# Causal mask of an attention: added by VectorE while it finds the row maxima, in place of mask matmuls on TensorE

## The chip, the core and the metric

The kernel runs on one core of one Trainium2 chip. The metric is the device time of one execution in microseconds (us). The core has four computing engines that each work through their own list of instructions in order, and wait for one another by semaphores: TensorE (PE in the profile: matmuls, and its weight loads as PEld), VectorE (DVE), ScalarE (ACT), GpSimd (POOL). DMA queues are fed by SyncE (SP) and by GpSimd. TensorE writes only to PSUM; the other data lie in SBUF.

## The reference, cut to what matters

One decoder layer on x (8 batches x 512 rows x 256 columns): a first attention without softmax, then a causal attention with 16 heads of 64, then 16 experts with 4 chosen per row. The change is in the second:

```python
qh = (q @ Wq.T + bq)...; kh = (k @ Wk.T + bk)...; vh = (v @ Wv.T + bv)...   # b, 16 heads, 512, 64
scores = einsum('bhqd,bhkd->bhqk', qh, kh) / sqrt(64)
causal = tril(ones((512, 512), bool))
scores = where(causal, scores, -inf)
attn   = softmax(scores, axis=-1)
out    = einsum('bhqk,bhkd->bhqd', attn, vh) ...  @ Wo.T + bo
```

## The kernel before

The whole layer is one program. It has three stages: the first attention (to about 209 us of the span), the causal attention (to about 1131 us), and the experts (to the end). The change is in the causal attention.

**Pairs.** The causal attention goes over 64 pairs of heads (8 batches, 8 pairs each; n counts the pairs). The two heads of a pair are called even and odd. The 512 rows of a head are four tiles of 128 rows; row tile i needs only the first (i+1)*128 columns of scores. The tiles are taken in blocks, `BLOCKS = (3, 2, 1)`: block 3 is row tile 3 (512 columns), block 2 is row tile 2 (384), block 1 is row tiles 1 and 0 (256 and 128).

**Order.** `attention_plan` writes out one list of steps, and every engine goes through that list and takes its own part of each step. For a pair n the list is, in short: scores of blocks 3 and 2; the transposes ("turn", five groups of four, L1286) of the probabilities of pair n-1, with "soften" of blocks 3 and 2 between them; "even" of blocks 3 and 2; the projections of k, v and q for pair n+1; scores and soften of block 1; steps of the routing or of the next batch ("middle"); "even" of block 1; further steps ("second"); "weigh" (probabilities times v, L1298) and "keep" of pair n-1. Then the scores of pair n+1 follow.

**One block on the engines.** "scores" (TensorE, L1269): six matmuls per row tile, since each product is made of three terms with high and low parts, for two heads; then four mask matmuls (L1274), in which an identity and a mask (zero on and below the diagonal, -1e30 above it, both bf16, held twice for the two halves of the array) add the mask to the last 128 columns in PSUM. "soften": VectorE finds the negated row maxima of both heads in one `tensor_reduce` per row tile (L1526), straight from PSUM; ScalarE takes the exponentials from PSUM with that bias, writes them to `prob` in SBUF and collects the row sums (L1400, one per head and row tile, each with an instruction that reads the accumulator). "even": VectorE inverts the sums (L1533) and scales `prob` in place (L1538). The transposes of pair n wait for "even" of block 1 of pair n (signal `s_norm`).

**Banks.** Scores use two PSUM slots `SB` of two banks, in turn: block after block. Before the change the scores of a block wait until the exponentials of the block two before have been read out (`s_exp`). All other products share four `work` banks, each free again when VectorE or ScalarE has emptied it.

**Around it.** k and q of a pair are split in a high part (ScalarE, L1383 and L1385) and a low part (VectorE, L1515 and L1519) before their scores. In some pairs VectorE has more between soften and even of block 1: `norm3` (L1485) in pair 2 of a batch, `place` (L1642 to L1657) and `lower_x` (L1508) in pair 6. In the first attention VectorE copies identity and mask into their two halves (`repeat_halves`, L748 and L749).

## Time and profile before

| | |
|---|---|
| time, median of 3 runs | 1635.06 us (1634.19 to 1638.66) |
| span of the profiled execution | 1636.8 us |
| PE busy | 1574.4 us (96%) |
| PE weight loads busy | 1329.4 us (81%) |
| DVE busy | 1164.3 us (71%) |
| ACT busy | 1077.0 us (66%) |
| POOL busy | 524.1 us (32%) |
| mask matmuls, L1274 | 1024 |
| row maxima, L1526 | 256, 198.1 us busy |
| exponentials, L1400 | 512, 265.9 us busy, and 512 accumulator reads, 108.8 us |

The profile gives no other time for the profiled execution than its span; it lies between the lowest and the highest of the three runs, 1.7 us over their median. "Busy" adds up the durations of instructions; on TensorE neighbouring matmuls overlap, so what one of them costs is read from start to start and not from its own duration.

### The profile page before, as it was taken

To read this page: it belongs to the slowest core of one execution; us is meant where nothing else is said; L and a number is where in the kernel's file an instruction comes from. 1 tells how busy PE (TensorE), PEld (TensorE's weight loads), DVE (VectorE), ACT (ScalarE), POOL (GpSimd) and SP (SyncE) were. 2 spreads that over 40 slices of the span, in tenths; PEclk is the share of its full clock that TensorE was granted. 3 is DMA by queue.
4 is the path that set the end of the run, shared out by engine and by line. 5 is a ranking of instruction groups with operands and counts; after the bars stand their busy time and mean duration, and the time that the engine had idled before them with its cause. 6 is when DMAs were issued, how large, how long until landed. Compare 5 with 4: busy or idle time off the path is not lost.

```text
span 1636.8 us, 35892 instructions
## 1 busy us (share of the span) xinstructions
PE 1574.4 (96%) x12438; PEld 1329.4 (81%) x12438; DVE 1164.3 (71%) x2745; ACT 1077.0 (66%) x2702; POOL 524.1 (32%) x440
## 2 busy tenths in 40 slices
PE   5999989999999999999999999997999999999997
PEld 4888867777777777777777777776999999999997
DVE  6877767676767677677677777777886666666663
ACT  3555557666766676676676667666776677677675
POOL 3444400000310300301202102104567745655655
PEclk9999999999999999999999999999999999999999
DMA  3122194044292490580730302046778887777874
GB/s 102 39 90 78 40 267 127 1 130 144 72 286 67 143 272 11 174 250 18 227 111 36 101 1 80 15 136 205 162 182 206 200 200 173 175 181 171 176 180 49
DMA packets 164610, 216.14 MB, mean 132 GB/s; under 512 B 16672, under 2 KB 124752, under 8 KB 164432
## 3 DMA queue, kind: packets, MB, share of 16 engines
q1 hardware_dynamic: 134080, 173.77, 35.2%
q0 software_dynamic: 28896, 38.62, 12.7%
q8 instruction: 103, 1.69, 0.4%
q10 hardware_dynamic: 1456, 1.44, 0.3%
q14 instruction: 75, 0.61, 0.1%
HBM read 90.76 MB, written 123.03 MB: 131 GB/s over the span
## 4 chain that ended last, share of the span: by engine, by line
PE 69%; ACT 14%; DVE 11%; issue 4%; DMA 1%; POOL 0%; SPq 0%; DVEq 0%; ACTq 0%
PE ex_H L1836 14%; PE ex_Y L1850 13%; ACT xa_prob L1400 7%; PE xa_work L1315 6%; PE xa_work L1240 5%; PE xa_work L1298 5%; PE xa_S L1269 5%; PE xa_work L1286 5%; PE xa_work L1251 4%; ACT xa_probT L1414 4%; PE a_work L458 4%; PE ex_X L1818 2%; DVE xa_nmax L1526 2%; DVE xa_prob L1538 2%; ACT xa_probT L1411 1%
## 5 line engine op out<-in xcount | busy, mean ns | idle before, releaser
L1400 ACT ACTIVATE xa_prob<-xa_S,xa_nmax 128x512 f32<-128x512 f32 (+3 forms) x512 | 265.9, 534 | 115.2 <-DVE xa_nmax L1526 97.6
L1943 POOL DMA_INDIRECT out<-ex_y,ahead_bits x158 | 272.8, 1727 | 200.7 <-POOLq L1939 73.6
L1836 PE MATMUL ex_H<-ex_xT,ex_w 128*128 128x256 f32 x1896 | 245.8, 286 | 5.9 <-issue 3.2
L1836 PEld LDWEIGHTS ex_H<-ex_xT,ex_w 128*128 128x128 f32 x1896 | 231.5, 191 | 6.8 <-issue 6.7
L1850 PE MATMUL ex_Y<-experts_w_hi,ex_hT 128*128 x1264 | 236.6, 280 | 0.2 <-issue 0.2
L1526 DVE TENSOR_REDUCE xa_nmax<-xa_S 128x2 f32<-128x1024 f32 (+3 forms) x256 | 198.1, 816 | 4.7 <-PE xa_S L1274 4.7
L1850 PEld LDWEIGHTS ex_Y<-experts_w_hi,ex_hT 128*128 128x128 f32 x1264 | 198.7, 188 | 0.5 <-issue 0.5
L1711 POOL DMA_INDIRECT expert_rows<-kept_xn,kept_rows x112 | 111.1, 992 | 266.6 <-DVE xa_prob L1538 224.2
L1921 DVE TENSOR_TENSOR ex_hT<-ex_h,ex_hT 128x512 fp32r<-128x512 f32 x158 | 108.2, 692 | 120.4 <-ACT ex_hT L1875 116.6
L1414 ACT ACTIVATE xa_probT<-xa_work 128x512 f32<-128x512 f32 x256 | 139.6, 603 | 81.9 <-PE xa_work L1286 73.4
L1850 PE MATMUL ex_Y<-experts_w_lo,ex_hT 128*128 x632 | 176.3, 279 | 0.0
L1538 DVE TENSOR_SCALAR xa_prob<-xa_prob,xa_sums 128x512 f32<-128x512 f32 (+3 forms) x512 | 169.3, 384 | 6.8
L1870 ACT ACTIVATE ex_h<-ex_H,kept_b 128x256 f32<-128x256 f32 x316 | 131.2, 466 | 63.6 <-DVE kept_b L1909 47.8
L1286 PE MATMUL xa_work<-ahead_ident,xa_prob 128*128 128x128 f32 x1280 | 155.4, 277 | 8.5 <-DVE xa_prob L1538 7.1
L1298 PE MATMUL xa_work<-xa_probT,xa_v 128*64 128x512 f32 (+3 forms) x1024 | 153.5, 442 | 2.2 <-ACT xa_probT L1411 2.2
L1286 PEld LDWEIGHTS xa_work<-ahead_ident,xa_prob 128*128 128x128 f32 x1280 | 139.4, 142 | 15.8 <-DVE xa_prob L1538 10.2
L1298 PEld LDWEIGHTS xa_work<-xa_probT,xa_v 128*64 128x64 f32 x1024 | 68.2, 137 | 82.9 <-issue 67.0
L1883 ACT ACTIVATE ex_y<-ex_Y,ahead_bits 128x256 f32<-128x256 f32 x158 | 73.9, 473 | 77.4 <-PE ex_Y L1850 57.0
L1533 DVE RECIPROCAL xa_sums<-xa_sums 128x2 f32<-128x2 f32 (+1 forms) x192 | 32.1, 167 | 128.4 <-ACT xa_prob L1400 128.3
L1850 PEld LDWEIGHTS ex_Y<-experts_w_lo,ex_hT 128*128 128x128 f32 x632 | 118.6, 188 | 0.0
L1400 ACT ACTIVATION_READ_ACCUMULATOR xa_prob<-xa_S,xa_nmax 128x1 f32 x512 | 108.8, 213 | 0.0
L1875 ACT ACTIVATE ex_hT<-ex_h 128x512 fp32r<-128x512 f32 x158 | 99.9, 632 | 5.0
(384 smaller groups left out, 3587.6 us busy)
## 6 DMA issues: line engine op xcount, KB each, us to landing
expert_rows<-xa_room_of_w_hi_and SPq DMA_DIRECT2D x256, 273.0 KB
kept_x<-expert_rows SPq DMA_DIRECT2D x52, 273.0 KB
ex_w_raw<-in_w SPq DMA_DIRECT2D x27, 512.0 KB
ahead_ctx<-in_w SPq DMA_DIRECT2D x26, 512.0 KB
ahead_x<-in_w SPq DMA_DIRECT2D x26, 512.0 KB
kept_xn<-expert_rows SPq DMA_DIRECT2D x27, 273.0 KB
experts_w_lo<-in_w SPq DMA_DIRECT2D x6, 1024.0 KB, 5.5
expert_rows<-xa_room_of_w_hi_and SPq DMA_DIRECT2D x32, 136.5 KB
```

The costliest lines, as they stand in the source:

```text
L1286: m = pe.transpose(PJ[:, col:col + P], prob[n % 2][:, odd, PROB_AT[i] + j * P:PROB_AT[i] + (j + 1) * P], ident[:])
L1298: m = pe.matmul(OB[HD * odd:HD * odd + HD, j * P:512], v[n % 2][:, j, first_col + HD * odd:first_col + HD * odd + HD], probT[:, odd, PROB_ ...
L1400: m = act.activation(prob[n % 2][:, odd, PROB_AT[i]:PROB_AT[i] + width], SB[slot[at]][:, odd, col:col + width], ACT.Exp, bias=nmax[n % 2][ ...
L1414: act.activation(probT[:, odd, first_col:first_col + 512], bank(step, at)[:], ACT.Copy).then_inc(t_ev.of(at), 1)
L1526: m = dve.tensor_reduce(nmax[n % 2][:, i, :], SB[slot[at]][:, :, SCORE_COL[i]:SCORE_COL[i] + (i + 1) * P], AX.X, ALU.max, negate=True)
L1538: m = dve.tensor_scalar(part, part, sums[n % 2][:, i, odd:odd + 1], None, ALU.mult)
L1711: pool.indirect_dma_start(rows_dram, bass.IndirectOffsetOnAxis(rows_i[b % 2][:, t, k:k + 1], 0), xn3[:, t, :], None).then_inc(scattered[of ...
L1836: m = pe.matmul(bank[:, (f % 2) * ROWS:(f % 2 + 1) * ROWS], ww[:, c, f * P:(f + 1) * P], xx[:, c, :], start=(i == 0), stop=(i == len(terms ...
L1850: m = pe.matmul(YB[a][:, 0:D], hh[:, f, a * P:(a + 1) * P], W2[:, bass.ds(own * WE + f * D, D)], start=(i == 0), stop=(i == len(terms) - 1))
L1870: i = act.activation(h32[:, f, :], HB[2 * (j % 2) + u][:, (f % 2) * ROWS:(f % 2 + 1) * ROWS], ACT.Gelu, bias=b1[j % 2][:, f:f + 1])
L1921: dve.tensor_tensor(hT[j % 2][1][:, fs, :], h32[:, fs, :], f32(hT[j % 2][0][:, fs, :]), op=ALU.subtract).then_inc(h_lo.of((j, u)), 1)
L1943: pool.indirect_dma_start(out, bass.IndirectOffsetOnAxis(tail[j % NT][:, a, 0:1].bitcast(I32), 0), y[j % NY][:, a, :], None, compute_op=AL ...
```

## The change

TensorE no longer adds the mask: the four mask matmuls of each row tile go, and the third term's matmul ends the group. The mask is now one bf16 tile of 128 x 512 that is zero but for its last 128 columns; a row tile of some width takes the last `width` columns of it. "soften" on VectorE becomes one `tensor_tensor_reduce` per head and row tile (8 per pair, in place of 4 reductions): it reads the scores from PSUM and the mask from SBUF, writes -(score + mask) to `prob`, and gives the minimum over the row, which is the negated maximum. ScalarE then takes the exponentials in place in `prob`, in SBUF, with scale -1. The PSUM slot is free when VectorE is through (`s_max`), not when ScalarE is. `s_pe` and `s_max` are waited for head by head. The identity and mask copies of the first attention go; GpSimd fills one mask.

```diff
-        self.ident_of, self.mask_of, self.tri, self.onesb = (self.bits[:, at, :] for at in (slice(0, 2), slice(2, 4), 4, 5))
+        self.mask, self.tri, self.onesb = self.bits[:, 0:N_TILES, :].rearrange("p t n -> p (t n)"), self.bits[:, 4, :], self.bits[:, 5, :]
...
-            def repeat_halves():
-                w.wait_ge(mask_set, "maskb")
-                for odd in range(2):
-                    for half_ in range(2):
-                        mine, theirs = slice(HD * odd, HD * odd + HD), slice(HD * half_, HD * half_ + HD)
-                        dve.tensor_copy(ahead.ident_of[mine, half_, :], identb[theirs])
-                        i = dve.tensor_copy(ahead.mask_of[mine, half_, :], maskb[theirs])
-                i.then_inc(halves_set.of(0), 1)
+            def scale_bq():
                 w.wait_ge(small_in, "rb")
...
+            pool.affine_select(out=ahead.mask[:, S - P:S], in_=ahead.mask[:, S - P:S], compare_op=ALU.is_ge, fill=NEG, base=0,
+                               pattern=[[-1, P]], channel_multiplier=1).then_inc(mask_set.of("mask"), 1)
...
+        mask_of, tri, onesb = lambda width: ahead.mask[:, S - width:S], ahead.tri, ahead.onesb
...
                 if at in before_in_slot:
-                    w.wait_ge(s_exp, (*before_in_slot[at], 1))
+                    w.wait_ge(s_max, (*before_in_slot[at], 1))
...
-                            pe.matmul(bank_pair[:, odd, col:col + n_cols], qq[mine, i * P:(i + 1) * P], kk[mine, 0:n_cols],
-                                      start=(term == 0), stop=False)
-                    for half in range(2):
-                        for odd in range(2):
-                            mine, skipped = slice(HD * odd, HD * odd + HD), HD * half
-                            m = pe.matmul(bank_pair[:, odd, col + width - P + skipped:col + width], ident_of[mine, half, :],
-                                          mask_of[mine, half, skipped:P], start=False, stop=(half == 1))
-                            if half == 1 and i == ROWS_OF[blk][-1]:
+                            m = pe.matmul(bank_pair[:, odd, col:col + n_cols], qq[mine, i * P:(i + 1) * P], kk[mine, 0:n_cols],
+                                          start=(term == 0), stop=(term == 2))
+                            if term == 2 and i == ROWS_OF[blk][-1]:
                                 m.then_inc(s_pe.of((n, blk, odd)), 1)
...
             elif step == "soften":                      # ScalarE
                 n, blk = at
-                w.wait_ge(t_pe, (n - 2, len(TURNS) - 1), n >= 2)
-                w.wait_ge(s_norm, (n - 2, 1), n >= 2)
-                w.wait_ge(Wo_lo, 0, n == 1)
-                w.wait_ge(s_max, at)
+                w.wait_ge(s_inv, (n - 2, 1), n >= 2)
                 for odd in range(2):
+                    w.wait_ge(s_max, (n, blk, odd))
                     for i in ROWS_OF[blk]:
-                        col, width = SCORE_COL[i], (i + 1) * P
-                        m = act.activation(prob[n % 2][:, odd, PROB_AT[i]:PROB_AT[i] + width],
-                                           SB[slot[at]][:, odd, col:col + width], ACT.Exp,
-                                           bias=nmax[n % 2][:, i, odd:odd + 1], accum_out=sums[n % 2][:, i, odd:odd + 1])
+                        part = prob[n % 2][:, odd, PROB_AT[i]:PROB_AT[i] + (i + 1) * P]
+                        m = act.activation(part, part, ACT.Exp, scale=-1.0, bias=nmax[n % 2][:, i, odd:odd + 1],
+                                           accum_out=sums[n % 2][:, i, odd:odd + 1])
...
             elif step == "soften":                      # VectorE
                 n, blk = at
                 w.wait_ge(s_exp, (n - 2, 1, 1), n >= 2)
-                w.wait_ge(s_pe, (n, blk, 1))
-                for i in ROWS_OF[blk]:
-                    m = dve.tensor_reduce(nmax[n % 2][:, i, :], SB[slot[at]][:, :, SCORE_COL[i]:SCORE_COL[i] + (i + 1) * P],
-                                          AX.X, ALU.max, negate=True)
-                m.then_inc(s_max.of(at), 1)
+                w.wait_ge(t_pe, (n - 2, len(TURNS) - 1), n >= 2)
+                w.wait_ge(Wo_lo, 0, n == 1)
+                for odd in range(2):
+                    w.wait_ge(s_pe, (n, blk, odd))
+                    for i in ROWS_OF[blk]:
+                        col, width = SCORE_COL[i], (i + 1) * P
+                        m = dve.tensor_tensor_reduce(prob[n % 2][:, odd, PROB_AT[i]:PROB_AT[i] + width],
+                                                     SB[slot[at]][:, odd, col:col + width], mask_of(width), scale=-1.0, scalar=-NEG,
+                                                     op0=ALU.add, op1=ALU.min, accum_out=nmax[n % 2][:, i, odd:odd + 1])
+                    m.then_inc(s_max.of((n, blk, odd)), 1)
```

Line numbers of the kernel after are lower by 8 to 17 in the causal attention. On TensorE, block 1 of one pair stands so before (`xa_S` are the scores in PSUM, `ahead_bits` holds identity and mask):

```order
L1269 MATMUL xa_S<-xa_k0hi,xa_q0lo 128x256 x2
L1269 MATMUL xa_S<-xa_k0lo,xa_q0hi 128x256 x2
L1269 MATMUL xa_S<-xa_k0hi,xa_q0hi 128x256 x2
L1274 MATMUL xa_S<-ahead_bits 128x128 x2
L1274 MATMUL xa_S<-ahead_bits 128x64 x2
L1269 MATMUL xa_S<-xa_k0hi,xa_q0lo 128x256 x2
L1269 MATMUL xa_S<-xa_k0lo,xa_q0hi 128x256 x2
L1269 MATMUL xa_S<-xa_k0hi,xa_q0hi 128x256 x2
L1274 MATMUL xa_S<-ahead_bits 128x128 x2
L1274 MATMUL xa_S<-ahead_bits 128x64 x2
```

and so after:

```order
L1260 MATMUL xa_S<-xa_k0hi,xa_q0lo 128x256 x2
L1260 MATMUL xa_S<-xa_k0lo,xa_q0hi 128x256 x2
L1260 MATMUL xa_S<-xa_k0hi,xa_q0hi 128x256 x2
L1260 MATMUL xa_S<-xa_k0hi,xa_q0lo 128x256 x2
L1260 MATMUL xa_S<-xa_k0lo,xa_q0hi 128x256 x2
L1260 MATMUL xa_S<-xa_k0hi,xa_q0hi 128x256 x2
```

Only the mask matmuls are gone; the rest keeps its order. On VectorE, in pair 6 of a batch, the stretch from the low part of q to the inverse sums of block 1 stands so before (`xa_nmax` are the negated maxima, `xa_pos` to `kept_rows` is the step `place`):

```order
L1519 SCALAR_TENSOR_TENSOR xa_q1lo<-xa_work,ahead_bqT,xa_q1hi 128x512
L1526 TENSOR_REDUCE xa_nmax<-xa_S 128x2 x2
L1642 TENSOR_TENSOR xa_pos<-xa_work,routing_count 128x64
L1645 TENSOR_TENSOR routing_count<-xa_work,routing_count 128x16
L1647 TENSOR_TENSOR xa_key<-xa_pos,ahead_ebase 128x64
L1650 TENSOR_TENSOR xa_key<-xa_key,xa_mask 128x64
L1653 MAX xa_key<-xa_key 128x8 x4
L1657 TENSOR_SCALAR kept_rows<-xa_key 128x16
L1508 TENSOR_TENSOR ahead_xT_lo<-xa_work,ahead_xT_hi 128x512
L1533 RECIPROCAL xa_sums<-xa_sums 128x4
```

and its beginning after:

```order
L1502 SCALAR_TENSOR_TENSOR xa_q1lo<-xa_work,ahead_bqT,xa_q1hi 128x512
L1513 ISA xa_prob,xa_nmax<-xa_S,ahead_bits 128x256
L1513 ISA xa_nmax 128x1
L1513 ISA xa_prob,xa_nmax<-xa_S,ahead_bits 128x128
L1513 ISA xa_nmax 128x1
L1513 ISA xa_prob,xa_nmax<-xa_S,ahead_bits 128x256
L1513 ISA xa_nmax 128x1
L1513 ISA xa_prob,xa_nmax<-xa_S,ahead_bits 128x128
L1513 ISA xa_nmax 128x1
L1630 TENSOR_TENSOR xa_pos<-xa_work,routing_count 128x64
```

Two reductions have become four `tensor_tensor_reduce`, and each of these is followed by an instruction of its own that writes only the 128x1 result. So soften of a pair has 16 instructions on VectorE where it had 4. ScalarE and GpSimd have the same order as before in this stage.

## Rows read from the trace of the kernel before

**Rows 1.** Stretch: length; busy PE, PEld, DVE, ACT, POOL; clock; DMA share; GB/s.
```profile
440.00:610.00 170.00, 168.35 (x1339) 126.92 (x1338) 123.80 (x313) 114.75 (x311) 30.76 (x31) 1.00 0.64 190
```

**Rows 2.** Waits of TensorE, whole span: us in total, times, longest us.
```profile
PE xa_work L1286 <- DVE xa_prob L1538: 7.1, 20, 1.0
```

**Rows 3.** Chain that ended last, from 712 us: start us, us, what.
```profile
718.33 0.10 PE xa_S L1274 x4
718.43 1.60 PE xa_work L1286 x13
```

**Rows 4.** The same chain, one pair from 240 us.
```profile
241.95 1.09 ACT xa_probT L1414 x2
...
248.85 0.75 DVE xa_q1lo L1519
249.60 0.94 DVE xa_nmax L1526 x2
...
250.56 1.73 ACT xa_prob L1400 x8
...
252.53 1.02 DVE xa_prob L1538 x4
...
253.59 0.67 PE xa_work L1286 x4
```

**Rows 5.** The same chain in pair 6 of a batch.
```profile
644.97 0.93 DVE xa_nmax L1526 x2
...
647.28 0.59 DVE ahead_xT_lo L1508
...
647.99 1.01 DVE xa_prob L1538 x4
```

**Rows 6.** Timeline of VectorE: start us, us, instructions, [idle before <- releaser].
```profile
646.66 0.41 DVE L1653 MAX8 xa_key<-xa_key 128x8 f32<-128x16 f32 x4
647.10 0.18 DVE L1657 TENSOR_SCALAR kept_rows<-xa_key 128x16 int32<-128x16 f32 x1
647.19 0.68 DVE L1508 TENSOR_TENSOR ahead_xT_lo<-xa_work,ahead_xT_hi 128x512 fp32r<-128x512 f32 x1
647.79 0.17 DVE L1533 RECIPROCAL xa_sums<-xa_sums 128x4 f32<-128x4 f32 x1
```

**Rows 7.** VectorE's groups by form: count, busy us, mean ns of one.
```profile
L1526 DVE TENSOR_REDUCE xa_nmax<-xa_S 128x2 f32<-128x1024 f32 x64 | 77.8, 1216 | 1.2 <-PE xa_S L1274 1.2
L1526 DVE TENSOR_REDUCE xa_nmax<-xa_S 128x2 f32<-128x256 f32 x64 | 26.6, 416 | 0.0
L1593 DVE MATCH_VALUE_LOAD xa_repl<-xa_top,ahead_probs 128x8 f32 x32 | 2.7, 85 | 0.3
```

**Rows 8.** ScalarE's groups by form.
```profile
L1400 ACT ACTIVATION_READ_ACCUMULATOR xa_prob<-xa_S,xa_nmax 128x1 f32 x512 | 108.8, 213 | 0.0
L563 ACT ACTIVATE a_sq<-a_sq_q 128x256 f32<-128x256 f32 x32 | 13.4, 418 | 1.0
L560 ACT ACTIVATE a_sq_q<-a_work 128x256 f32<-128x256 f32 x32 | 11.9, 372 | 0.0
```

**Rows 9.** Timeline of VectorE and TensorE at the turn of pairs.
```profile
717.10 1.01 DVE L1538 TENSOR_SCALAR xa_prob<-xa_prob,xa_sums 128x256 f32<-128x256 f32 x4
...
660.38 1.01 DVE L1538 TENSOR_SCALAR xa_prob<-xa_prob,xa_sums 128x256 f32<-128x256 f32 x4
...
662.13 2.08 PE L1286 MATMUL xa_work<-ahead_ident,xa_prob 128*128 128x128 f32 x17
```

**Rows 10.** Timeline of VectorE in pair 2 of a batch.
```profile
701.92 1.38 DVE L1485 TENSOR_SCALAR kept_xn<-xa_x,xa_ln_mv,xa_ln_rstd 128x256 f32<-128x256 f32 x4
703.79 0.18 DVE L1533 RECIPROCAL xa_sums<-xa_sums 128x4 f32<-128x4 f32 x1 [0.49 <-ACT xa_prob L1400]
```

**Rows 11.** Chain in the first attention: the first and last copy of the two halves.
```profile
70.27 0.09 DVE ahead_bits L748
...
71.28 0.10 DVE ahead_bits L749
```

More of the change, by code:

```diff
@@ L132, in __init__ @@
         self.b1 = [sb(f"b1_{i}", [P, FC]) for i in range(2)]
-        bits, wide = ahead.bits[:].rearrange("p a b -> p (a b)").bitcast(F32), RT * (PAY - D)
-        self.b1T, self.scr = bits[:, 0:E * FC], bits[:, 2 * P:2 * P + 6 * E].rearrange("p (i e) -> p i e", e=E)
-        self.tail = [bits[:, E * FC + i * wide:E * FC + (i + 1) * wide].rearrange("p (a c) -> p a c", a=RT) for i in range(NT)]
+        room, wide = ahead.bits[:].rearrange("p a b -> p (a b)").bitcast(F32), RT * (PAY - D)
+        self.b1T, self.scr = room[:, 0:E * FC], room[:, 2 * P:2 * P + 6 * E].rearrange("p (i e) -> p i e", e=E)
+        self.tail = [room[:, E * FC + i * wide:E * FC + (i + 1) * wide].rearrange("p (a c) -> p a c", a=RT) for i in range(NT)]
 class Tables:
@@ L305, in first_attention @@
         ones, half = sb("ones", [P, 2]), sb("half", [P, N_TILES])
-        identb, maskb = sb("identb", [P, P], BF16), sb("maskb", [P, P], BF16)
         b2, b2_hi = sb("b2", [P, D]), sb("b2_hi", [P, D], F32R)
@@ L362, in first_attention @@
         b2_zero, b2_in = signal("b2_zero", [0]), landed("b2_in", range(len(GATE_AT)))
-        b2_ready, halves_set = signal("b2_ready", ["cast", "hi", "lo"]), signal("halves_set", [0])
-        mask_set, bq_scaled, bo_added = signal("mask_set", ["fill", "identb", "maskb"]), signal("bq_scaled", [0]), signal("bo_added", [0])
+        b2_ready = signal("b2_ready", ["cast", "hi", "lo"])
+        mask_set, bq_scaled, bo_added = signal("mask_set", ["fill", "mask"]), signal("bq_scaled", [0]), signal("bo_added", [0])
         x_of = lambda b: x_in[b % 3] if b < B else ahead.x1_0
@@ L818, in vector @@
                 if b == 2:
-                    repeat_halves()
+                    scale_bq()
                 k = chunk_of(b)
@@ L892, in gpsimd @@
             pool.memset(b2[:], 0.0).then_inc(b2_zero.of(0), 1)
-            for tile, fill in ((identb, 0.0), (maskb, 0.0), (ahead.tri, 1.0), (ahead.onesb, 1.0)):
+            for tile, fill in ((ahead.mask, 0.0), (ahead.tri, 1.0), (ahead.onesb, 1.0)):
                 i = pool.memset(tile[:], fill)
@@ L943, in first_attention @@
         engines = {"tensor": tensor, "scalar": scalar, "vector": vector, "gpsimd": gpsimd, "sync": sync}
-        return engines, x1_stored, {"work_ev": work_ev, "bo_added": bo_added}
+        return engines, x1_stored, {"work_ev": work_ev, "bo_added": bo_added, "mask_set": mask_set}
 BLOCKS = (3, 2, 1)
@@ L1129, in cross_attention @@
         s_pe, s_exp = signal("s_pe", heads_of), signal("s_exp", heads_of)
-        s_max, s_inv, s_norm = (signal(n, of_scores) for n in ("s_max", "s_inv", "s_norm"))
+        s_max = signal("s_max", heads_of)
+        s_inv, s_norm = (signal(n, of_scores) for n in ("s_inv", "s_norm"))
         t_pe, t_ev = signal("t_pe", turns), signal("t_ev", turns)
```

5 lines of the change are left out of this document (removed).

## The prediction

> **What bounds the kernel now.** I read the stretches of busy time first. In the causal attention TensorE is busy 168.35 of 170 us, VectorE 123.80, ScalarE 114.75 [rows 1]. So taking work from TensorE should pay, if VectorE and ScalarE can follow. Whether they can is not in the shares, so I read TensorE's waits next: its first transpose of a pair (L1286) waited 20 times for VectorE's scaled probabilities (L1538), 7.1 us in all [rows 2]. Small, but there are only 63 such hand-overs, so at 20 of them the other two engines are already as late as TensorE. The chain of waits shows the path there: first transposes, then ScalarE from 241.95 without a pause until q is split, VectorE (low part of q at 248.85, maxima at 249.60), ScalarE (exponentials 250.56), VectorE (scaling 252.53), and the next pair's transposes at 253.59 [rows 4]. Such a pair is set by ScalarE and VectorE, not by TensorE.
>
> I sorted the 63 hand-overs by how long the probabilities had been ready when TensorE came for them; the batches repeat almost to 0.1 us. Class A, 13: TensorE waits, the chain is that of [rows 4]. Class B, 7 (pair 2 of a batch): the same, with `norm3` (L1485) on VectorE between the maxima and the inverse sums [rows 10]. Class C, 7 (pair 6, and the last pair but one): VectorE has no pause from the maxima at 644.97 through place and lower_x to the scaling at 647.99 [rows 5]. Class D, 6: ready at 717.10 + 1.01 = 718.11, wanted at 718.43 [rows 9, 3]: 0.3 us to spare. Class E, 30: at least 0.7 us to spare; the tightest is ready at 661.39 and wanted at 662.13 [rows 9].
>
> **The change part by part.**
>
> *Mask matmuls.* Four of them hold the path for 0.10 us (718.33 to 718.43) [rows 3]; their own durations overlap and say nothing. 256 row tiles make 25.6 us, 0.40 us a pair. That is all TensorE can give back. In class E all of it is gained.
>
> *Row maxima.* Two things have to be sized. A two-input instruction over 512 columns from PSUM takes 0.60 us from its start to the next start (647.19 to 647.79) [rows 6]. The slope of the present reductions is (1216 - 416) / 768 = 1.04 ns a column [rows 7]; so 0.60, 0.47, 0.33 and 0.20 us for 512, 384, 256 and 128 columns. Then the separate instruction that writes the 128x1 minimum. VectorE has no such one in this trace. The nearest are small ones: MATCH_VALUE_LOAD takes 85 ns itself [rows 7], four MAX8 take 0.44 us from start to start (646.66 to 647.10), 0.11 each [rows 6]; ScalarE's accumulator read has 213 ns [rows 8]. From below it could be hidden altogether (0), from above it is 0.21. I take 0.10, as MAX8 is an instruction of the same engine. Block 1 then needs 2 x (0.33 + 0.20) + 4 x 0.10 = 1.46 us on VectorE in place of 0.93 [rows 5]; but ScalarE may begin after one head. Before, it began 0.96 after the maxima (249.60 to 250.56) [rows 4]; now about 0.73 plus the read's tail, 0.8: 0.2 us sooner. Blocks 3 and 2 cost VectorE 2 x 1.07 + 0.4 = 2.54 us in place of 2.0; ScalarE can start block 3 some 0.07 sooner. The unknown of the sum is what one of the 8 instructions with its read costs beyond this.
>
> *Exponentials.* From SBUF in place of PSUM. A ScalarE instruction of 256 columns with an accumulator takes 418 ns from SBUF (L563) and 372 from PSUM (L560) [rows 8]: 0.045 more each, 0.18 for four. In classes A to C eight of them lie on the path of a pair, in D the last four. It could be nothing, if the difference is one of the function.
>
> *The PSUM slot* comes free after the minima and no longer after the exponentials. That helps no class by itself: in A to C the probabilities, not the slot, end the wait. The new waits of VectorE (transposes of pair n-2) and of ScalarE (inverse sums of pair n-2) are long met; behind a waiting VectorE would stand the scaling and the low parts of k and q.
>
> *The copies* in the first attention: eight, from 70.27 to 71.38 on the chain [rows 11], 1.1 us; later the chain runs into a transfer, so between 0 and 1.1; I take 0.6.
>
> Per hand-over this gives:
> - A: -0.20 (earlier start) + 0.18 + 0.18 (eight exponentials) - 0.07 = +0.09 us; 13 make 1.2 lost. TensorE's 0.40 is worth nothing here: it only waits longer.
> - B: VectorE is now late in place of ScalarE: 1.46 + 1.38 = 2.84 us from the first maximum to the inverse sums [rows 10], where ScalarE would have them after 0.8 + 1.73 + 0.18 + latency = 2.75 and before had them after 0.93 + 1.87 = 2.80 (701.92 to 703.79). +0.04 there, +0.11 in the first part of the pair: 0.15, 7 make 1.1 lost.
> - C: VectorE alone: 1.46 - 0.93 = 0.53, and 0.11 in ScalarE's part before it: 0.64, 7 make 4.5 lost.
> - D: 0.27 to spare after the latency, and 0.02 from the chain: 0.29 gained, 1.7 for 6.
> - E: 0.40, 12.0 for 30.
>
> Sum: 12.0 + 1.7 + 0.6 - 1.2 - 1.1 - 4.5 = 7.5 us gained of 25.6. The profiled execution's span of 1636.8 would become 1629.3. It stands 1.7 us over the median of the runs, so I set the gain against the median: 1635.1 - 7.5 = 1627.6 us. The experts' stage has none of these instructions and stays.
>
> The price of error is steep. For each us that an instruction with its read costs more, A and D lose 2 us a hand-over, B and C 4 (all four before the scaling): 26 + 12 + 28 + 28 = 94. So 0.08 us more each, and the gain is gone.
>
> **The rivals.**
>
> *1. Cheap minima.* The read is hidden: 0.10 less each. A gains 0.11 (1.4), B 0.14 until ScalarE is late again (1.0), C loses 0.24 (1.7), D and E 0.40 (14.4), copies 1.1: 16.2 gained, 1618.9 us. For it: ScalarE's own reads, 213 ns long, advance its chain by far less; 8 exponentials and reads take 1.73 us [rows 4]. Against: VectorE's smallest instructions all take some 0.1.
>
> *2. Everything TensorE gives back.* 63 x 0.40 + 1.1 = 26.3, 1608.8 us. It needs slack in the 20 hand-overs where TensorE waits now [rows 2]. I hardly believe it.
>
> *3. No overlap, no change.* The two instructions do not overlap as present neighbours do: 0.68 long but 0.60 to the next start [rows 6]. 0.08 each, 94 x 0.08 = 7.5 lost: 1635.1 us. The Trainium skill (VectorE: DVE Perf Modes, section The DRAIN you can't avoid) says that the next operation does not start until the pipe is empty, and advises to keep the count of operations low; by that rule alone this case would be the forecast, and it speaks against a change that makes 16 instructions of 4. The trace does not agree with it for ordinary neighbours.
>
> *4. VectorE becomes the bound.* The read costs as much as ScalarE's 0.21, and the new instruction, of a kind that the trace lacks, some 0.05 to 0.1 more than an ordinary two-input one: 0.16 to 0.21 each. 94 x 0.19 = 17.9 lost against 7.5: 1645.5 us. The place is block 1 of pairs 2 and 6 and the pairs like [rows 4]; it is slower than no change from 0.08 each, by over 0.3% from 0.13. VectorE's 16 instructions a pair stand for it; that its share would still be near 85% stands against a general jam, not against these places.
>
> *5. Half rate.* The instruction runs at two cycles a column: 1280 columns x 2 heads x 1.04 ns = 2.7 us more a pair. VectorE has 123.80 of 170 us [rows 1], 10.4 of a pair's 14.3, so it would be full, and all classes lose; roughly 30 us slower, 1665. For it nothing in the trace: its two-input instruction with one input in PSUM takes 0.60 us for 512 columns with all that is fixed in it [rows 6], which leaves no room for two cycles a column at the reductions' 1.04 ns a cycle. The Trainium skill (Vector Engine (DVE) Microarchitecture Reference, section Points that are easy to get wrong) says that a two-source instruction with an accumulator runs at half rate if both sources are non-bf16 and in SBUF; here the mask is bf16 and the scores are in PSUM, so by its own words it does not apply; no run here shows it.
>
> **How the numbers follow.** Chances: forecast 0.43, rival 1 0.17, rival 2 0.05, rival 3 0.15, rival 4 0.17, rival 5 0.03. 0.3% is 4.9 us, about what a measurement of this kernel can tell from no change. The forecast's own spread (a read of 0.06 to 0.14) is 1624 to 1631.5, so a quarter of it falls within 0.3%. Faster: 0.05 + 0.17 + 0.32 = 0.54. Same: 0.11 + 0.15 and a little of rival 4, 0.27. Slower: 0.19. The range goes from rival 1 with some of rival 2 to the middle of rival 4: 1616 to 1644.
>
> **What would show it.** Right: TensorE's waits for the scaled probabilities grow from 7.1 us to some 15 to 20, since it saves 0.4 us and gets it back in classes A to C; pairs of class E become 0.4 us shorter; the new instruction is near 0.69 and 0.29 us for 512 and 128 columns, its read near 0.15 in itself and 0.10 from start to start; exponentials 0.04 longer than before. In class C VectorE has no pause before the scaling and it comes later by 0.5 us. Wrong: first the start-to-start time of the new pair of instructions. If it is over 0.18 beyond the plain two-input one, the kernel is slower or the same. If the exponentials are not longer, A gains 0.3 a hand-over, 4 us more.

## The result and the profile after

The changed kernel takes 1611.22 us (median of 4 runs, 1608.31 to 1615.61), the kernel before in the same comparison 1635.65 us (1634.19 to 1638.66). The ratio is 0.9849, 95% interval 0.9829 to 0.9869. The forecast was 1627.6 us with a range down to 1616: the direction was right, the size was not. 24.4 us were gained where 7.5 were forecast. The profiled execution has a span of 1613.9 us against 1636.8, 22.9 us less.

The stretches of busy time after (length; busy PE, PEld, DVE, ACT, POOL; clock; DMA share; GB/s) answer to [rows 1]:

```profile
440.00:610.00 170.00, 167.44 (x1190) 127.23 (x1186) 131.14 (x472) 120.25 (x317) 28.04 (x28) 1.00 0.76 191
```

VectorE is busier (131.14 of 170 us, before 123.80), and so it is idle for less. TensorE's waits (us in total, times, longest) answer to [rows 2]:

```profile
PE xa_work L1272 <- DVE xa_prob L1526: 16.7, 28, 2.2
```

16.7 us in place of 7.1. This is inside the 15 to 20 that the forecast gave as the sign that it was right. It is no such sign: a wait grows when the awaited engines get slower, and also when TensorE gets faster by more than they do. The table of hand-overs below shows the second: where TensorE waits (A and B) the hand-overs became shorter, not longer.

VectorE's and ScalarE's new groups by form (count | busy us, mean ns of one):

```profile
L1513 DVE CUSTOM_DVE_ANT_0 xa_prob<-xa_S,ahead_bits 128x512 f32<-128x512 f32 x128 | 82.7, 683 | 1.1 <-PE xa_S L1260 1.1
L1513 DVE CUSTOM_DVE_ANT_0 xa_prob<-xa_S,ahead_bits 128x128 f32<-128x128 f32 x128 | 36.6, 286 | 0.0
L1513 DVE DVE_READ_ACCUMULATOR2_ANT xa_nmax<- 128x1 f32 x512 | 42.5, 83 | 0.0
L1384 ACT ACTIVATE xa_prob<-xa_prob,xa_nmax 128x512 f32<-128x512 f32 x128 | 91.4, 722 | 1.9 <-DVE xa_nmax L1513 1.9
L1384 ACT ACTIVATE xa_prob<-xa_prob,xa_nmax 128x128 f32<-128x128 f32 x128 | 49.6, 387 | 0.0
```

The new instruction takes 683 and 286 ns, as forecast (0.69 and 0.29). Its read takes 83 ns. What it costs the next one stands in the timeline. VectorE after, block 1 of the pair that answers to [rows 4] (start us, us, instruction):

```profile
247.60 0.75 DVE L1502 SCALAR_TENSOR_TENSOR xa_q1lo<-xa_work,ahead_bqT,xa_q1hi 128x512 fp32r<-128x512 f32 x1 [0.31 <-ACT xa_q1hi L1371]
248.27 0.41 DVE L1513 CUSTOM_DVE_ANT_0 xa_prob<-xa_S,ahead_bits 128x256 f32<-128x256 f32 x1
248.61 0.08 DVE L1513 DVE_READ_ACCUMULATOR2_ANT xa_nmax<- 128x1 f32 x1
248.61 0.28 DVE L1513 CUSTOM_DVE_ANT_0 xa_prob<-xa_S,ahead_bits 128x128 f32<-128x128 f32 x1
248.82 0.08 DVE L1513 DVE_READ_ACCUMULATOR2_ANT xa_nmax<- 128x1 f32 x1
...
249.38 0.08 DVE L1513 DVE_READ_ACCUMULATOR2_ANT xa_nmax<- 128x1 f32 x1
250.84 0.18 DVE L1521 RECIPROCAL xa_sums<-xa_sums 128x4 f32<-128x4 f32 x1 [1.37 <-ACT xa_prob L1384]
251.05 1.01 DVE L1526 TENSOR_SCALAR xa_prob<-xa_prob,xa_sums 128x256 f32<-128x256 f32 x4
```

The read starts at 248.61, and so does the next reduction. It costs no start-to-start time at all. All four take 249.38 - 248.27 = 1.11 us, where the forecast had 1.46.

ScalarE in the same block, first after and then before:

```profile
248.94 0.51 ACT L1384 ACTIVATE xa_prob<-xa_prob,xa_nmax 128x256 f32<-128x256 f32 x1 [1.37 <-DVE xa_nmax L1513]
```

```profile
250.56 0.47 ACT L1400 ACTIVATE xa_prob<-xa_S,xa_nmax 128x256 f32<-128x256 f32 x1 [1.75 <-DVE xa_nmax L1526]
```

and VectorE's maxima there before:

```profile
249.51 1.01 DVE L1526 TENSOR_REDUCE xa_nmax<-xa_S 128x2 f32<-128x512 f32 x2
```

Before, ScalarE began 250.56 - 249.51 = 1.05 us after the maxima. Now it begins 248.94 - 248.27 = 0.67 us after them: 0.38 sooner. The forecast had 0.2. It had read 249.60 as the start of the maxima from the chain [rows 4], which puts an instruction where its neighbour's duration ends; the timeline has 249.51.

TensorE's block 1, before and then after:

```profile
712.92 0.27 PE L1269 MATMUL xa_S<-xa_k1hi,xa_q1hi 64*128 64x256 f32 x2
713.04 0.26 PE L1274 MATMUL xa_S<-ahead_bits 64*128 64x128 bf16 x4
713.13 0.36 PE L1269 MATMUL xa_S<-xa_k1hi,xa_q1lo 64*128 64x256 f32 x2
713.34 0.28 PE L1269 MATMUL xa_S<-xa_k1lo,xa_q1hi 64*128 64x256 f32 x2
```

```profile
656.81 0.29 PE L1260 MATMUL xa_S<-xa_k0hi,xa_q0hi 64*128 64x256 f32 x2
656.93 0.29 PE L1260 MATMUL xa_S<-xa_k0hi,xa_q0lo 64*128 64x256 f32 x2
657.04 0.29 PE L1260 MATMUL xa_S<-xa_k0lo,xa_q0hi 64*128 64x256 f32 x2
```

The mask matmuls take 0.09 us, and the first matmul behind them 0.21 (713.13 to 713.34), where it takes 0.11 (656.93 to 657.04) behind one of its own kind. So a row tile's mask costs some 0.19 where another row tile follows at once. Over the blocks of a pair TensorE saves 0.28 us in blocks 3 and 2 (start of the scores to the start of what follows, 1.70 to 1.42) and 0.28 in block 1 (1.19 to 0.91): 0.56 us a pair, not 0.40.

**All hand-overs.** The table gives, for every kernel run here, the mean time from a pair's first transpose to the next pair's, by the prediction's classes, read from the timelines of TensorE. Class A is split into first pairs of a batch (A0, 7) and others (A1, 6); one of class E's 30 is the first and has no cycle. The sum is from the first of the 63 hand-overs to the last.

```
kernel                         A1 (6)  A0 (7)  B (7)   C (7)   D (6)   E (29)  sum us
before                         12.41   12.74   12.18   12.06   13.29   16.08   879.4
after                          12.13   12.02   12.01   12.33   12.81   15.56   855.4
e1  before, no mask matmuls    12.44   12.22   12.19   12.02   13.07   15.63   861.4
e5  before, heads apart        11.94   12.25   11.82   12.15   13.13   15.97   867.2
e6  before, both               11.85   11.78   11.78   12.16   12.58   15.49   846.0
e2  after, mask matmuls back   12.18   12.54   12.04   12.33   13.26   16.19   880.6
e3  after, small op added      12.27   12.14   12.14   12.57   12.93   15.57   860.7
e4  after, both heads first    13.13   12.83   12.64   12.37   13.62   15.81   883.8
e7  after, slot by exps        12.13   12.02   12.01   12.33   12.81   15.56   855.5
e8  after, exps from PSUM      11.88   11.80   11.80   12.21   12.58   15.50   846.9
e9  after, signal a row tile   11.92   11.81   11.85   12.33   12.70   15.54   850.4
e10 e9, later lower_x          11.99   11.80   11.84   11.92   12.69   15.59   849.2
e11 after, run once more       12.13   12.02   12.01   12.33   12.81   15.57   855.5
e12 after, masked in PSUM      11.99   11.91   11.91   12.32   12.64   15.51   850.6
```

The sums can be compared from chip to chip: e11 is the changed kernel once more, on another chip than e7, and the two agree with the first profile to 0.1 us. What a whole execution takes varies more than that, mostly outside this stretch, so the sums tell finer differences than the ratios do; where the two disagree, both are given below.

Of the 22.9 us between the two profiled executions 24.0 are in these hand-overs and 0.8 before them (the first at 226.58, before 227.35); behind them 1.8 to 1.9 are lost; that part varies by 5 us over the kernels run here. By class A gained 6.8 us where 1.2 were to be lost, B gained 1.1 where 1.1 were to be lost, C lost 1.9 and not 4.5, D gained 2.9 and not 1.7, E gained 15.1 and not 12.0.

### The profile page after: what moved, and what is told of

Its sections match the earlier page's. It is cut to its first block, busy times and chain, and to the rows that moved or that the text cites. A ratio compares the mean times of both kernels' runs of the same rounds, so it can differ in the third digit from the quotient of the medians.

```text
span 1613.9 us, 34663 instructions
## 1 busy us (share of the span) xinstructions
PE 1544.2 (96%) x11414; PEld 1308.3 (81%) x11414; DVE 1183.6 (73%) x3505; ACT 1089.1 (67%) x2702; POOL 528.8 (33%) x438
## 3 DMA queue, kind: packets, MB, share of 16 engines
q0 software_dynamic: 28896, 38.62, 13.1%
## 4 chain that ended last, share of the span: by engine, by line
PE 65%; ACT 15%; DVE 10%; issue 4%; DMA 4%; POOL 2%; POOLq 1%; SPq 0%; ACTq 0%; DVEq 0%
PE ex_H L1824 11%; PE ex_Y L1838 11%; ACT xa_prob L1384 7%; PE xa_work L1231 6%; PE xa_work L1284 6%; PE xa_work L1301 6%; PE xa_work L1272 6%; PE xa_S L1260 5%; PE a_work L457 4%; PE xa_work L1242 4%; ACT xa_probT L1397 4%; DMA out<-ex_y,ahead_bits 3%; DVE xa_prob L1526 2%; PE ex_X L1806 2%; POOL out L1931 1%
## 5 line engine op out<-in xcount | busy, mean ns | idle before, releaser
L1384 ACT ACTIVATE xa_prob<-xa_prob,xa_nmax 128x512 f32<-128x512 f32 (+3 forms) x512 | 282.7, 558 | 85.0 <-DVE xa_nmax L1513 85.0
L1513 DVE CUSTOM_DVE_ANT_0 xa_prob<-xa_S,ahead_bits 128x512 f32<-128x512 f32 (+3 forms) x512 | 219.4, 485 | 1.1 <-PE xa_S L1260 1.1
L1272 PE MATMUL xa_work<-ahead_ident,xa_prob 128*128 128x128 f32 x1280 | 158.0, 279 | 18.1 <-DVE xa_prob L1526 16.7
L1384 ACT ACTIVATION_READ_ACCUMULATOR xa_prob<-xa_prob,xa_nmax 128x1 f32 x512 | 99.5, 194 | 0.0
```

What stands on the lines that cost most here:

```text
L1272: m = pe.transpose(PJ[:, col:col + P], prob[n % 2][:, odd, PROB_AT[i] + j * P:PROB_AT[i] + (j + 1) * P], ident[:])
L1384: m = act.activation(part, part, ACT.Exp, scale=-1.0, bias=nmax[n % 2][:, i, odd:odd + 1], accum_out=sums[n % 2][:, i, odd:odd + 1])
L1513: m = dve.tensor_tensor_reduce(prob[n % 2][:, odd, PROB_AT[i]:PROB_AT[i] + width], SB[slot[at]][:, odd, col:col + width], mask_of(width), ...
```

## Experiments

Two theories were to be told apart. One: the gain is TensorE's, from its mask matmuls. Two: it comes from the chain of VectorE and ScalarE, which the change also starts head by head. Ratios are to the kernel before, run on the same chip.

**e1: the kernel before without its mask matmuls.** It leaves the mask out.

```diff
-                            pe.matmul(bank_pair[...], qq[...], kk[...], start=(term == 0), stop=False)
-                    for half in range(2):
-                        for odd in range(2):
...
-                            m = pe.matmul(bank_pair[...], ident_of[mine, half, :], mask_of[...], start=False, stop=(half == 1))
+                            m = pe.matmul(bank_pair[...], qq[...], kk[...], start=(term == 0), stop=(term == 2))
```

> The kernel before with the mask matmuls left out and nothing else changed (the causal mask is missing from the result). It gives TensorE's share alone. Theory 1 (TensorE gives back 0.56 us a pair, not 0.40, but only where it was late; elsewhere the hand-over chain of VectorE and ScalarE sets the time and is as long as before): 30 roomy hand-overs x 0.52 + 6 x 0.28 + some 0.6 = 17.9 us, about 1617.5 us, and the waits of the first transposes grow to over 15 us. Theory 2 (all of the gain is TensorE's, VectorE's new instructions bring and cost nothing): 1611 to 1612 us, as the changed kernel. Had TensorE's saving been 0.40 a pair as forecast: 12.0 + 1.7, about 1622 us.

Measured: 0.9863 (0.9839 to 0.9886), 18.0 us in the hand-overs. Of this 13.1 is in E, 3.7 in A0, 1.3 in D. The other A pairs gain nothing (12.41 to 12.44), nor do B and C: they are set by the chain, as forecast. The ratio alone would be 22.4 us of 1635.65, or 1613 us (1609 to 1617), which is nearer to theory 2; the kernel before was not profiled on that chip, so where the other 4 us lie is not known. It is the hand-overs by class that speak for theory 1: the changed kernel gains in A1 and B, this one doesn't. TensorE's wait there:

```profile
PE xa_work L1281 <- DVE xa_prob L1533: 13.4, 33, 1.1
```

**e2: the changed kernel with four matmuls per row tile back that add a zero part of the mask.**

```diff
+                            m = pe.matmul(bank_pair[...], ahead.mask[mine, 0:P], ahead.mask[mine, S - P + skipped:S], start=False, stop=(half == 1))
```

> The changed kernel with four mask-shaped matmuls per row tile put back on TensorE; they multiply a block of zeros by the mask and add nothing. The result is the same, VectorE and ScalarE keep the new way. Theory 1: the 36 hand-overs where TensorE is now late lose 0.5 to 0.56 us each, the others have the wait to hide it: +18 to +20 us, about 1630.5 us, so VectorE's and ScalarE's way alone is worth some 5 us. Theory 2: 1635 to 1636 us, as before the change. The forecast's own price (0.40 a pair): about 1624.5 us.

Measured: 0.9952 (0.9932 to 0.9972), so by the ratios 1.0% (17 us) of the gain is gone. In the profiled execution it is all gone, 25.2 us. Of this 5.1 is the clock and not the matmuls: every second batch took 115 us and the others 113.5, and in each of the three long ones TensorE's granted clock fell from 1.00 (2.4 GHz) to 0.50 (1.2 GHz) for some 3.4 us, near 500, 729 and 957 us, after it had been busy without a pause. Two stretches (columns as in [rows 1]), then the 16 "weigh" matmuls in the second of them, and in the batch behind it:

```profile
490.00:500.00 10.00, 10.00 (x84) 8.60 (x84) 8.54 (x26) 8.19 (x21) 0.00 (x0) 1.00 1.09 309
500.00:503.00 3.00, 3.00 (x10) 0.99 (x12) 1.85 (x8) 1.08 (x6) 0.00 (x0) 0.50 0.16 45
...
499.97 4.00 PE xa_work L1289 x16
...
615.13 2.38 PE L1289 MATMUL xa_work<-xa_probT,xa_v 128*64 128x512 f32 x16
```

Each such pair took 15.23 us, its like in the next batch 13.54. Without them the matmuls cost 20.1 us in the hand-overs, where theory 1 had 18 to 20. E loses 0.63 (0.46 without the clock) and D 0.45, A0 0.52, while A1, B and C lose nothing (12.18 for 12.13). So e1 and e2 agree on where the mask matmuls count, and that they are worth 17 to 20 us.

**e5: the kernel before with the maxima head by head, and a signal for each head.** The mask matmuls and the exponentials from PSUM stay.

```diff
-                w.wait_ge(s_pe, (n, blk, 1))
-                for i in ROWS_OF[blk]:
-                    m = dve.tensor_reduce(nmax[n % 2][:, i, :], SB[slot[at]][:, :, ...], AX.X, ALU.max, negate=True)
-                m.then_inc(s_max.of(at), 1)
+                for odd in range(2):
+                    w.wait_ge(s_pe, (n, blk, odd))
+                    for i in ROWS_OF[blk]:
+                        m = dve.tensor_reduce(nmax[n % 2][:, i, odd:odd + 1], SB[slot[at]][:, odd, ...], AX.X, ALU.max, negate=True)
+                    m.then_inc(s_max.of((n, blk, odd)), 1)
```

> The kernel before, mask matmuls and exponentials from PSUM as they were, but the maxima are found one head at a time (8 reductions a pair in place of 4) and ScalarE starts after the first head. The first four runs say that TensorE's mask matmuls hold most of the time, and that the start after one head is what keeps the hand-overs from eating it. Theory 1: with TensorE still as slow, the hand-overs that wait (20) gain at most their wait of 0.3 to 0.4 us and those with place lose 0.2: about 3 us faster than before (1632 where before is 1635; ratio 0.998). Rival (the early start is worth much by itself): ratio 0.993 or lower.

Measured: 0.9939 (0.9921 to 0.9957), 12.2 us in the hand-overs. That is near the rival's number (0.993) and four times the 3 us of theory 1. A1 gains 0.47, A0 0.49, B 0.36, D 0.16, E 0.11, and C loses 0.09. The wait of [rows 2] is nearly gone:

```profile
PE xa_work L1287 <- DVE xa_prob L1540: 1.9, 2, 1.5
```

Its reductions by form:

```profile
L1528 DVE TENSOR_REDUCE xa_nmax<-xa_S 128x1 f32<-128x512 f32 x128 | 81.8, 680 | 1.2 <-PE xa_S L1275 1.2
```

A plain reduction over 512 columns takes 680 ns and the new one, with mask and minimum, 683. From start to start it is 0.598 us here and 0.606 in the changed kernel. Adding the mask costs VectorE some 0.01 us.

**e6: e1 and e5 together.**

> The same, with the mask matmuls left out too (the causal mask is missing from the result): all that the change gives, without the exponentials in place in SBUF and with plain reductions. Theory 1: TensorE's 0.56 a pair counts in nearly every hand-over, and ScalarE's chain is 0.34 a pair shorter than in the changed kernel: ratio to before 0.982, some 5 us faster than the changed kernel. If the place of the scores (SBUF or PSUM) and the new instruction cost nothing: as the changed kernel, 0.985.

Measured: 0.9789 (0.9772 to 0.9807), 33.4 us in the hand-overs; 18.0 + 12.2 = 30.2 by the single runs. The two gains are independent but for 3 us, and 2.0 of these are in D (13.29 to 12.58), the class with little to spare: what TensorE saves there is worth more when the chain is shorter too. This kernel leaves the mask out and stands 9.4 us in the hand-overs below the changed kernel, where 5 were expected.

**e4: the changed kernel, with ScalarE waiting for both heads' maxima.**

```diff
+                w.wait_ge(s_max, (n, blk, 1))
                 for odd in range(2):
-                    w.wait_ge(s_max, (n, blk, odd))
```

> The changed kernel, but ScalarE starts the exponentials of a block only when the minima of both heads are there, as in the kernel before. Theory 1: the start after one head is worth 0.55 us in block 1 wherever the chain of VectorE and ScalarE sets the hand-over (13 x 0.75 + 7 x 0.7 + 7 x 0.2 + 6 x 0.5 = 19 us): about 1630 us. Theory 2 (TensorE alone sets the time): no change, 1611 us.

Measured: 1.0000 (0.9983 to 1.0018). The whole gain is gone, with the mask matmuls away: 24.7 us by the ratios, 28.4 in the hand-overs, where theory 1 had 19. One of the A1 pairs has a stretch at the lower clock (0.57 in the mean of 242 to 246 us) and takes 1.0 longer for it; the one behind it takes 12.83, where the changed kernel has 12.02: 0.55 later exponentials in block 1, as theory 1 had it, and 0.26 more in the first part of the pair. TensorE's waits:

```profile
PE xa_work L1272 <- DVE xa_prob L1526: 35.7, 36, 2.3
...
PE xa_work L1242 <- ACT xa_probT L1397: 5.7, 29, 0.5
```

The first has doubled. The second is new: ScalarE's copies of transposed groups stand behind its late exponentials, and TensorE, which shares the four `work` banks with them, waits for the copies. ScalarE and TensorE in the pair at 256.56 us:

```profile
259.20 0.71 ACT L1384 ACTIVATE xa_prob<-xa_prob,xa_nmax 128x512 f32<-128x512 f32 x1
259.81 0.19 ACT L1384 ACTIVATION_READ_ACCUMULATOR xa_prob<-xa_prob,xa_nmax 128x1 f32 x1
259.90 1.05 ACT L1397 ACTIVATE xa_probT<-xa_work 128x512 f32<-128x512 f32 x2
...
260.53 0.50 PE L1242 MATMUL xa_work<-WvT_hi,ahead_cT_lo 128*128 128x512 f32 x1 [0.18 <-ACT xa_probT L1397]
```

So neither theory alone. In the changed kernel both parts are needed, and the signals by head, a side of the change, weigh as much as the mask matmuls (28.4 us of hand-overs in e4, 20.1 in e2); added to the kernel before the change they weigh less (12.2 in e5, against 18.0 in e1).

**e3: the changed kernel with one 128x1 operation more behind each of the 8 reductions of a pair** (4 instructions for each head's blocks 3, 2 and 1; they write a spare place).

```diff
+                        m = dve.tensor_scalar(room[:, 8 + 4 * odd + i:9 + 4 * odd + i], ident[:, 0:1], 1.0, None, ALU.mult)
```

> The changed kernel with one more small VectorE instruction (128x1) after each of the 8 tensor_tensor_reduce of a pair. It puts back the 0.10 us that the forecast had charged for each read of the accumulator, and which the trace shows at 0. By the forecast's slope of 94 us per us each: +9.4 us, about 1620.6 us. If the slope is right, the read's price explains more than half of the miss. Rival: VectorE's time is not what sets the hand-overs now; then under 3 us.

Measured: 0.9861 (0.9839 to 0.9882), 5.3 us more in the hand-overs than the changed kernel. The ratios put it only 2 us above the changed kernel and their intervals overlap, so by the time alone the rival (under 3 us) would stand; that the cost is real rests on the hand-overs, where A, B and D lose 0.12 to 0.14 us each and C 0.24. The timeline of VectorE:

```profile
249.08 0.41 DVE L1514 CUSTOM_DVE_ANT_0 xa_prob<-xa_S,ahead_bits 128x256 f32<-128x256 f32 x1
249.42 0.08 DVE L1514 DVE_READ_ACCUMULATOR2_ANT xa_nmax<- 128x1 f32 x1
249.42 0.15 DVE L1517 TENSOR_SCALAR xa_room_in_front_of_w<-ahead_ident 128x1 f32<-128x1 f32 x1
249.49 0.28 DVE L1514 CUSTOM_DVE_ANT_0 xa_prob<-xa_S,ahead_bits 128x128 f32<-128x128 f32 x1
```

The added operation is 0.15 us long and takes 0.07 from start to start (249.42 to 249.49). 5.3 / 0.066 (the mean of such steps) is 80 us for each us. The forecast's slope was 94: right within a fifth. It was multiplied with a wrong price.

**e7: the changed kernel, the PSUM slot free only after the exponentials.**

```diff
-                    w.wait_ge(s_max, (*before_in_slot[at], 1))
+                    w.wait_ge(s_exp, (*before_in_slot[at], 1))
```

> The changed kernel, but TensorE waits for the exponentials of the block that had a PSUM slot before, as in the kernel before, and not for the minima. Theory: the slot's earlier release is worth nothing, since the scores of block 2 come 2.5 us after the low part of q and the exponentials end at 2.44: ratio to before as the changed kernel, 0.985, at most 1 us slower. Rival (the earlier release is what lets TensorE keep its 0.56 a pair): 5 us or more slower, ratio 0.988 or higher.

Measured: 0.9866 (0.9844 to 0.9888), and the hand-overs agree with the changed kernel's to 0.1 us in their sum. The earlier slot is worth nothing, as forecast.

**e8: e7 with the exponentials reading the scores from PSUM.** They read unmasked scores, so this kernel leaves the mask out of the probabilities.

> The changed kernel with the exponentials read from PSUM (without the mask, so the result is not causal) and the slot waited for by the exponentials; VectorE still writes the masked scores. It prices SBUF against PSUM for ScalarE. Theory: 0.34 us a pair less on ScalarE's chain, which counts in the 13 hand-overs that the chain sets, and in part in the 6 with little to spare and the 14 with more on VectorE: 5 to 7 us faster than the changed kernel, ratio to before 0.981. Rival: ScalarE's longer instructions are covered: 0.985.

Measured: 0.9798 (0.9782 to 0.9815), 8.7 us less than e7 in the hand-overs, where 5 to 7 were expected. The exponentials by form:

```profile
L1384 ACT ACTIVATE xa_prob<-xa_S,xa_nmax 128x512 f32<-128x512 f32 x128 | 87.3, 697 | 1.9 <-DVE xa_nmax L1513 1.9
L1384 ACT ACTIVATE xa_prob<-xa_S,xa_nmax 128x128 f32<-128x128 f32 x128 | 46.8, 366 | 0.0
```

697 and 366 ns from PSUM, 722 and 387 from SBUF: 21 to 25 ns longer in themselves (with 384 columns only 2 ns, 621 for 619). From start to start four of block 1 take 1.77 us (248.94 to 250.71) and in e8 1.61 (247.59 to 249.20), 0.04 each, as the forecast had it (0.045); it is 0.04 for each of the four widths, also for 384 columns (0.60 for 0.56).

**e9 to e11: one step further.** e9 gives the signal after each row tile's reduction; e10 also moves the transposes and low parts of the coming x in pair 6 behind "even" of block 1 (into "second"), where half of them stood ahead of it; e11 is the changed kernel again, beside them.

```diff
                     for i in ROWS_OF[blk]:
+                        w.wait_ge(s_max, (n, blk, odd, i))          # ScalarE
...
+                        m.then_inc(s_max.of((n, blk, odd, i)), 1)   # VectorE
```

> The changed kernel, with VectorE's signal of a head's maxima given after each of its row tiles, so that ScalarE's first exponential waits for one reduction and not for two. Theory (the wait for ScalarE's start is on the path of the 12.1 us hand-overs and of the 12.81 us ones): the start comes one reduction earlier, 0.21 us in block 1 (145.78 to 145.99 starts of this kind), so 13 + 6 hand-overs x 0.21 = 4.0 us less, 0.9975 of the changed kernel. In the first of each block 1 pair ScalarE is still busy with the turn copies for part of this, so half of it is a possible outcome: 2 us. Rival (ScalarE's own queue decides, since the second exponential waits for its own reduction anyway): no difference, within 0.5 us.

> As the run before, and in the seventh pair of each batch the transposes of the coming x and VectorE's low parts of them for both halves stand after the scores of that pair, instead of one half of each ahead of the maxima. Theory (VectorE's queue ahead of the maxima is what is late in the seventh pair, the 12.3 us hand-overs): 7 hand-overs x about 0.3 us = 2 us less than the run before. Rival: the low parts are then late for the projections and the same time is lost there; no difference or up to 2 us more.

> The changed kernel once more, beside the two runs before it, to compare them on one chip: 0.985 of the kernel before, as first measured (0.983 to 0.987).

Measured: e9 1609.71 us, 0.9813 (0.9797 to 0.9829); e10 1610.60, 0.9829 (0.9812 to 0.9845); e11 1614.43, 0.9846 (0.9824 to 0.9868). In the hand-overs e9 gains 5.1 us over the changed kernel (4.0 expected). ScalarE starts 0.21 sooner after the maxima in block 1, as expected (248.22 to 248.68, in the changed kernel 248.27 to 248.94); its first exponential in e9:

```profile
248.68 0.51 ACT L1384 ACTIVATE xa_prob<-xa_prob,xa_nmax 128x256 f32<-128x256 f32 x1 [1.16 <-DVE xa_nmax L1513]
```

e10 gains 0.41 in each C pair and gives 0.05 back in E: 1.1 us in the sum where 2 were expected, which its times don't show. The intervals of e9 and e11 overlap a little; the sums of the hand-overs don't leave a doubt about the direction.

**e12: the changed kernel with the masked scores written back to PSUM**, the exponentials read there; the whole computation is kept.

```diff
-                        m = dve.tensor_tensor_reduce(prob[n % 2][:, odd, PROB_AT[i]:PROB_AT[i] + width],
+                        m = dve.tensor_tensor_reduce(SB[slot[at]][:, odd, col:col + width],
...
-                        m = act.activation(part, part, ACT.Exp, scale=-1.0, ...
+                        m = act.activation(part, SB[slot[at]][:, odd, ...], ACT.Exp, scale=-1.0, ...
```

> The changed kernel, with the masked scores written over the scores in PSUM in place of the probabilities' buffer; the exponentials read PSUM as in the kernel before, the whole mask is kept, and TensorE waits for the exponentials before it overwrites a slot. Theory (the price of the change is where ScalarE reads: without a mask in the reread scores the same route gave 846.85 us of hand-overs against 855.54): again about 847 us, some 8 us less than the changed kernel, ratio 0.980, if a reduction that writes PSUM is as fast as one that writes SBUF (683 ns). Rival: it is slower by the difference of a VectorE operation with both ends in PSUM; each 0.1 us of it for a 512-wide reduction delays the chain of a pair by 0.1 to 0.4 us, so that at 0.1 us and more the gain is gone: 855 us or more, ratio 0.985 to 0.99.

Measured: 1612.59 us beside 1645.07, 0.9801 (0.9776 to 0.9826), 4.9 us less than the changed kernel in the hand-overs and not 8. The reductions:

```profile
L1513 DVE CUSTOM_DVE_ANT_0 xa_S<-xa_S,ahead_bits 128x512 f32<-128x512 f32 x128 | 85.7, 712 | 1.1 <-PE xa_S L1260 1.1
L1513 DVE DVE_READ_ACCUMULATOR2_ANT xa_nmax<- 128x1 f32 x512 | 73.5, 144 | 0.0
```

and their timeline:

```profile
647.91 0.73 DVE L1513 CUSTOM_DVE_ANT_0 xa_S<-xa_S,ahead_bits 128x512 f32<-128x512 f32 x1
648.56 0.14 DVE L1513 DVE_READ_ACCUMULATOR2_ANT xa_nmax<- 128x1 f32 x1
648.56 0.60 DVE L1513 CUSTOM_DVE_ANT_0 xa_S<-xa_S,ahead_bits 128x384 f32<-128x384 f32 x1
649.07 0.14 DVE L1513 DVE_READ_ACCUMULATOR2_ANT xa_nmax<- 128x1 f32 x1
```

With both ends in PSUM this 512-wide one takes 0.65 from start to start and not 0.61, the 384-wide 0.51 and not 0.48; the first 512-wide one of the two heads takes 0.61 in both kernels. So most reductions cost 0.04 us more, where reading PSUM saves ScalarE 0.04 for each exponential: half of the gain remains. e9, e10 and e12 all lie below the changed kernel, by 0.2 to 0.45 points of ratio, and all below the kernel before; which of them is best these runs don't tell.

## Why the prediction was wrong

The mechanism was read rightly in the main: TensorE bounds class E, the chain of ScalarE and VectorE bounds A1, B and C. e1, which changes TensorE alone, leaves A1, B and C as they were; e5, which changes the chain alone, has 8.8 of its 12.2 us in A and B. Three sizes and one sorting were wrong, all in one direction.

- **The read of the minimum**, "I take 0.10", costs 0. This is the step that failed. At 80 us per us (e3) it is 8 us, nearly half of the missing 17. The trace before held the clue and the forecast named it in its rival 1: ScalarE's reads are 213 ns long [rows 8] and advance its own chain by 0.1 only (here 259.81 to 259.90 in e4). MAX8, from which the value was taken, is a full operation, not a read.
- **ScalarE's earlier start**, 0.20 us in block 1, was 0.38; block 3's, 0.07, was 0.17 (the exponentials begin 0.97 us after the first turn copies, 240.79 to 241.76, and began 1.14 after them, 241.95 to 243.09). Of the first, 0.09 is the chain's 249.60, and 0.13 that ScalarE had to wait 0.67 and not 0.8, since the two reads cost nothing.
- **The mask matmuls**, 0.10 us a row tile, were 0.14: the 0.10 was read at 718.33, where the next matmuls are of another stage. Behind the others the next fp32 matmul is 0.10 late as well. "That is all TensorE can give back" (25.6 us) was too low: it is 0.56 x 64 = 36 us. In class E it was worth 15.1 us and not 12.0.
- **First pairs of a batch** were put in class A, but they gain 0.72 us each, and 0.52 from the mask matmuls alone (e1; e2 loses the same 0.52). VectorE waits there for the scores before:

```profile
670.87 1.02 DVE L1526 TENSOR_REDUCE xa_nmax<-xa_S 128x2 f32<-128x512 f32 x2 [0.56 <-PE xa_S L1274]
```

The classes were sorted by who waited at the end of a pair, and this wait in its middle was not looked for. It goes with the mask matmuls: it is in 6 of the 7 pairs before, in 3 of 7 in e5 and in 1 of 7 in e2, which all have them, and in none in the kernels without them. In the other four of e5 TensorE itself is late: it comes 0.5 us after the scaled probabilities. So these pairs stood on the edge between TensorE and the chain, and not on the chain's side. Why the scores' signal came so late stays open: the last mask matmuls start at 669.73, over 1 us earlier. The 0.52 make 3.6 of the missing us.

What was right: the exponentials from SBUF (0.18 in each half of a pair, some 8 us by the forecast's classes; e7 and e8 give 8.7), the slot (nothing; e7), VectorE's own time for the two-input reductions, the slope, and that classes A1 and B don't gain from the mask matmuls. The copies (0.6) were not shown either way: the first hand-over came 0.8 us sooner, but it scatters from 225.4 to 229.1 over the kernels run here. C was to lose 0.64 and lost 0.27: without four reads of 0.10 the forecast would have been 0.24.

Of the rivals, 2 comes nearest to the measured time (1608.8) for the wrong reason, by luck: it let every hand-over give TensorE's 0.40. In fact E gives 0.52, and A1 and B give 0.28 and 0.17 from the chain. Rival 1 (16.2 us) is the mechanism that was the case, short of the mis-sized mask matmuls and the A0 pairs. Rivals 3 to 5 are out. The reductions overlap as present neighbours do: one of 0.68 us is followed after 0.61 (0.41 after 0.34 at 248.27), and its read by the next at once. The trace does not agree with the rule that rival 3 names. But that section of the Trainium skill (VectorE: DVE Perf Modes, section The DRAIN you can't avoid) itself adds that a next operation which is not held starts earlier, so it never spoke as plainly against this change as rival 3 has it. The advice to keep operations few stands in its section Rules for kernel authors; here 16 instructions in place of 4 did no harm. For rival 4 the read would have to cost 0.21 and it costs 0; for rival 5 a 512-wide reduction would have to take some 1.1 us and it takes 0.61.

## What to carry to other kernels

An accumulator's read was not an operation here: it cost 0 from start to start on VectorE and 0.1 on ScalarE. Price it from such a read, on another engine if need be, start to start, and not from the smallest operation of the same engine. Take starts from the timeline, not from the chain, and the cost of an instruction up to the second start behind it, since a change of kind can charge the next one. When an edit rewrites the signals as well, count them as a change of their own: here they alone were worth 0.6% (e5), and without them the changed kernel gained nothing (e4), though the mask matmuls alone are worth 18 us of hand-overs (e1): its longer reductions and exponentials ate that up. Before a batch that takes longer than its neighbours is put down to the kernel, look at the granted clock there.
